# Merging two gathered 64x64 layers: M in eight 64x32 tiles, W1 turned in two column tiles, x's products in half units

## The reference

```python
def cond(x, index, weights):                       # x (128, 64, 512)
    return jnp.einsum('bct,bcd->bdt', x, weights[index])
x = x + cond(x, itok_B_0_7, L0_cond_weights)       # 8 x 64 x 64
x = x + cond(x, itok_B_1_198, L1_cond_weights)     # 200 x 64 x 64
```

## Time and profile before

| | |
|---|---|
| median of 3 runs | 99.78 us (99.7 to 100.39) |
| the profiled execution | 100.29 us, of which the span is 97.4 us |
| PE busy | 69.0 us (71%) |
| DVE busy | 67.6 us (69%) |
| ACT busy | 54.8 us (56%) |
| POOL busy | 31.8 us (33%) |
| DMA | 35.90 MB, mean 369 GB/s |

### The profile page before, as it was taken

The page is one execution under the profiler, slowest core; times in us unless marked ns, Lnnn a source line. Parts: engine busy times, 40 slices in busy tenths (PEclk is TensorE's granted clock), DMA queues, the critical chain, the costliest instruction groups (busy, mean ns, idle before and its releaser), DMA issues.

```text
span 97.4 us, 2078 instructions
## 1 busy us (share of the span) xinstructions
PE 69.0 (71%) x708; PEld 37.3 (38%) x708; DVE 67.6 (69%) x111; ACT 54.8 (56%) x105; POOL 31.8 (33%) x135
## 2 busy tenths in 40 slices
PE   0400007997799999699699699979969969998000
PEld 0200006996782382265147138236414613322000
DVE  4293000588088889979979988997997997977900
ACT  2200000356277689759939938965992993955800
POOL 2400001888788788787758300000000000000000
PEclk9999999999999999999999999999999999999965
DMA  1999999999999999999999999999998984877975
GB/s 25 339 416 453 422 412 410 410 407 416 405 409 405 410 407 409 409 407 405 407 405 408 372 407 410 405 410 406 401 407 346 391 303 167 314 274 274 380 278 203
DMA packets 13243, 35.90 MB, mean 369 GB/s; under 512 B 689, under 2 KB 818, under 8 KB 13106
## 3 DMA queue, kind: packets, MB, share of 16 engines
q1 hardware_dynamic: 12944, 33.56, 88.5%
q0 software_dynamic: 144, 2.10, 5.0%
q10 hardware_dynamic: 146, 0.13, 0.4%
HBM read 19.01 MB, written 16.78 MB: 367 GB/s over the span
## 4 chain that ended last, share of the span: by engine, by line
PE 37%; DVE 34%; DMA 14%; issue 8%; DVEq 1%
PE psum L202 28%; DVE xy L242 21%; DVE m L236 12%; DMA w_rows<-in_L_cond_weights_dram,cond 12%; PE psum L171 8%; DMA cond<-in_itok_B_dram 3%; PE psum L183 2%; DVE w L222 1%; DVEq L58 1%; DVE w_rows L276 0%
## 5 line engine op out<-in xcount | busy, mean ns | idle before, releaser
L242 DVE COPY xy<-psum 64x512 f32<-64x512 f32 x64 | 43.8, 684 | 7.5 <-PE psum L202 5.8
L202 PE MATMUL psum<-xy,m 32*64 32x512 f32 x512 | 44.6, 600 | 5.1 <-DVE xy L242 5.1
L242 ACT COPY xy<-psum 64x512 f32<-64x512 f32 x64 | 37.2, 582 | 15.2 <-PE psum L202 13.8
L151 POOL COPY w0t_diag<-w0t 64x64 f32 x128 | 30.0, 234 | 19.9 <-issue 12.6
L202 PEld LDWEIGHTS psum<-xy,m 32*64 32x64 f32 x512 | 14.2, 130 | 29.9 <-DVE xy L242 18.4
L183 PEld LDWEIGHTS psum<-w,w0t_diag 128*128 128x128 f32 x128 | 14.8, 192 | 6.4 <-POOL w0t_diag L151 2.4
L183 PE MATMUL psum<-w,w0t_diag 128*128 128x64 f32 x128 | 15.7, 277 | 1.3 <-DVE w L222 1.3
L171 PE MATMUL psum<-ident,w_rows 128*64 128x128 f32 x64 | 8.5, 301 | 10.7 <-DVE w_rows L276 10.7
L236 DVE COPY m<-psum 32x256 f32<-32x256 f32 x32 | 13.3, 416 | 3.7 <-PE psum L183 2.8
L222 ACT COPY w<-psum 64x512 f32<-64x512 f32 x8 | 4.6, 578 | 17.3 <-PE psum L171 17.3
L236 ACT COPY m<-psum 32x256 f32<-32x256 f32 x32 | 11.7, 365 | 3.1 <-PE psum L183 2.4
(11 more groups left out here) (5 smaller groups left out, 0.6 us busy)
## 6 DMA issues: line engine op xcount, KB each, us to landing
xy<-in_x_dram SPq DMA_DIRECT2D x16, 1024.0 KB, 19.5
out_dram<-xy SPq DMA_DIRECT2D x16, 1024.0 KB, 8.6
w_rows<-in_L_cond_weights_dram ACTq DMA_DIRECT2D x1, 128.0 KB, 2.6
cond<-in_itok_B_dram SPq DMA_DIRECT2D x1, 0.5 KB, 2.5
subjects<-in_itok_B_dram ACTq DMA_DIRECT2D x1, 0.5 KB
w_rows<-in_L_cond_weights_dram,cond POOLq DMA_INDIRECT x1, 11.5
```

The source lines that it names most:

```text
L151: nc.gpsimd.tensor_copy(w0t_diag[rows, g % D_RING, n // 2, h * C:(h + 1) * C], w0t[rows, bass.ds(picked[n] * C, C)]).then_inc(s_w0_diag, 1)
L202: last = nc.tensor.matmul(psum[columns, (SLOT * v + r) % Y_BANKS, :], m[rows, g % M_RING, 2 * v + w - g * GROUP, j, :], xy[rows, 2 * v + w ...
L242: copy(xy[HALVES[r % 2], 2 * v + w, (r // 2) * T:(r // 2 + 1) * T], psum[HALVES[w], (SLOT * v + r) % Y_BANKS, :]).then_inc(done, 1)
```

## The change

POOL no longer writes blocks with zeros. It copies each batch's W0 as it is into `w0b` (128 copies of 64x64 again, no ring; a batch with odd = 0 on partitions 0 to 63, odd = 1 on 64 to 127, where odd is now which four of the unit's eight). DVE's two memsets go. W1 is turned by plain products with the identity as the moving operand, 64 columns each: 128 of them, half writing partitions 0 to 63 and half 64 to 127, so a turn comes out in one copy of 128 partitions. M of a batch is made in products of 64 rows, 32 columns, 64 moving: 16 to a unit on eight array tiles. M is taken out for a block of 1, 3, 4, 4 and 4 units (`BLOCKS`) by one copy on each of DVE and ACT. x's products come in steps of half a unit (8 products, four array tiles, one of three pairs of banks). `cond`'s DMA moves from SP's queue, ahead of x, to ACT's, ahead of W0. The list of registers for POOL is read before the wait for the gather.

```diff
-            for g in range(GROUPS):
-                if g >= D_RING:
-                    pool.wait_ge(s_m_psum, g - D_RING + 1)
...
+            for first in range(0, B, 2 * UNIT):
...
+                if first == 0:
+                    pool.wait_ge(s_gather, 16)
+                    pool.wait_ge(s_w0t, 4)
+                for n in range(2 * UNIT):
+                    v, odd, r = (first + n) // UNIT, n // SLOT % 2, n % SLOT
+                    nc.gpsimd.tensor_copy(w0b[HALVES[odd], v * SLOT + r, :],
+                                          w0t[HALVES[odd], bass.ds(picked[n] * C, C)]).then_inc(s_w0b, 1)
...
+            of = ident[:, :].rearrange("q (v o r) -> q o v r", o=2, r=SLOT)
...
-                    last = nc.tensor.transpose(psum[0:C, bank, (z % 4) * B:(z % 4 + 1) * B],
-                                               w1_rows[:, :, n * TURN + z], ident[:, :])
+                    for odd, rows in enumerate(HALVES):
+                        last = nc.tensor.matmul(psum[rows, n % W1_RING, z * C:(z + 1) * C],
+                                                w1_rows[:, :, n * TURN + z], of[:, odd, :, :],
+                                                start=True, stop=True)
...
+            def products(k):
+                first, n = BLOCKS[k]
+                pe.wait_ge(s_w0b, UNIT * (first + n))
+                if k >= 1:
+                    pe.wait_ge(s_m_v, k)
+                    pe.wait_ge(s_m_s, k)
+                for v in range(first, first + n):
+                    for j in range(J):
+                        for r in range(SLOT):
+                            for odd, rows in enumerate(HALVES):
+                                at = (v % M_COLUMNS * J + j) * C
+                                last = nc.tensor.matmul(psum[QUARTERS[r], M_BANK + odd, at:at + C],
+                                                        w0b[rows, v * SLOT + r, j * Q:(j + 1) * Q],
+                                                        w1[rows, v * SLOT + r, :], start=True, stop=True)
+                last.then_inc(s_m_psum, 1)
+            def apply(k):
+                first, n = BLOCKS[k]
...
+                for v in range(first, first + n):
+                    pe.wait_ge(s_x[v], 16)
+                    for a in range(2):
+                        step = 2 * v + a
+                        if step >= Y_RING:
+                            pe.wait_ge(s_y_v, 2 * (step - Y_RING + 1))
+                            pe.wait_ge(s_y_s, 2 * (step - Y_RING + 1))
+                        for j in range(J):
+                            for h in range(2):
+                                r = 2 * a + h
...
+                        last.then_inc(s_y_psum, 1)
...
+        def copy_y(eng, copy, done, odd, step):
+            v, a = step // 2, step % 2
+            eng.wait_ge(s_y_psum, step + 1)
+            if a == 0:
+                eng.wait_ge(s_y_psum, step + 2)
+            for h in range(2):
+                copy(xy[HALVES[h], 2 * v + odd, a * T:(a + 1) * T],
+                     psum[HALVES[odd], 2 * (step % Y_RING) + h, :]).then_inc(done, 1)
...
+            for k, (first, n) in enumerate(BLOCKS):
+                for step in range(2 * first, 2 * (first + n)):
+                    copy_y(eng, copy, y_done, odd, step)
+                if k + 2 < len(BLOCKS):
+                    copy_m(eng, copy, m_done, odd, k + 2)
```

More of the change, by code:

```diff
@@ L106, in _ @@
         def _(sp):
[L107 to L120, removed]
+            for v in range(UNITS):
+                sp.dma_start(xy[:, 2 * v:2 * v + 2, :], x_view[:, 2 * v:2 * v + 2, :]).then_inc(s_x[v], 16)
+            for v in range(UNITS):
+                sp.wait_ge(s_y_v, SLOT * (v + 1))
+                sp.wait_ge(s_y_s, SLOT * (v + 1))
+                sp.dma_start(out_view[:, SLOT * v:SLOT * (v + 1), :],
+                             xy[:, 2 * v:2 * v + 2, :].rearrange("q s (h t) -> q (s h) t", h=2)
+                             ).then_inc(s_out[v], 16)
+            for v in range(UNITS):
+                sp.wait_ge(s_out[v], 16)
         @block.gpsimd
@@ L173, in _ @@
                 last.then_inc(s_w1_turned, 1)
[L175 to L181, removed]
-                for k in range(GPAIRS):
-                    last = nc.tensor.matmul(psum[:, M_BANK + g % M_RING, k * C:(k + 1) * C],
-                                            w0t_diag[:, g % D_RING, k, :], w1[:, g * GPAIRS + k, :],
-                                            start=True, stop=True)
-                last.then_inc(s_m_psum, 1)
@@ new lines, in apply @@
+            def apply(k):
+                first, n = BLOCKS[k]
+                pe.wait_ge(s_m_v, k + 1)
+                pe.wait_ge(s_m_s, k + 1)
+                for v in range(first, first + n):
[8 more added lines that the diff above has]
+                                r = 2 * a + h
+                                for odd, columns in enumerate(HALVES):
+                                    last = nc.tensor.matmul(psum[columns, 2 * (step % Y_RING) + h, :],
+                                                            m[QUARTERS[r], odd, v % M_RING, j, :],
+                                                            xy[QUARTERS[r], 2 * v + odd, j * T:(j + 1) * T],
+                                                            start=j == 0, stop=j == J - 1)
+                        last.then_inc(s_y_psum, 1)
@@ new lines, in copies @@
+        def copies(eng, copy, w1_done, m_done, y_done, odd):
+            for n in range(odd, TURNS, 2):
+                copy_w1(eng, copy, w1_done, n)
+            copy_m(eng, copy, m_done, odd, 0)
+            copy_m(eng, copy, m_done, odd, 1)
+            for k, (first, n) in enumerate(BLOCKS):
[3 more added lines that the diff above has]
+                    copy_m(eng, copy, m_done, odd, k + 2)
```

116 lines of the change are left out of this document (32 added, 84 removed).

## The result

The changed kernel takes 110.25 us in the median (109.21 to 111.33), the kernel before 100.09 beside it; the ratio is 1.0995 (95% interval 1.088 to 1.111). Forecast were 98.0 us and at most 101.5. The profiled execution of the changed kernel took 111.33 us with a span of 109.5. Some executions of either kernel take longer, mostly at a lower mean granted clock (the profiled one is such a one, with 0.939 against 0.960 to 0.973 in the other three), and in this document medians count them while ratios leave them out.

A forecast was written before the change was run, and what follows sets the result against it. DVE and its hand-over to PE bound the kernel. Unit 1 at 38.9, 14 units of 3.48 and m copies reach 87.8; last copies 2.83, output 4.82: span 95.4, profiled 98.3, median 97.8, plus 0.2: 98.0 us (95.2 to 101.5).

The forecast's parts named there:

- The bound and the hand-over: Steady stage: DVE and its hand-over to PE bound it; period falls from 4.04 to 3.48 us a unit, M's copies nearly hidden.
- M's products in 64x32 tiles: M for four units: 128 records on eight tiles, 16 a tile at 0.057 us, so 0.9 us.
- the cover of 1.3: Steady stage: up to 1.3 us of M's products hide in PE's wait for DVE; anything past that delays the kernel.
- The rival built on it: M's 64x32 tiles overlap only in part: 3.6 us for four units, about 104.5 us in all; chance 0.12.
- 0.115 if the tiles overlap, 0.23 if not: W1's turning: us for a pair of 64-column products, two records on each of two tiles, against 0.106 a transpose before.
- my worst bound: W1's turning: 0.23 us for a pair of products if the two tiles do not overlap.
- a sign of being wrong: Start: the prediction called itself wrong if W1's turning lasts past 33 us.
- The wait for POOL: Start: PE waits about 5 us before M for block 2, until POOL's 64th copy, at 0.292 us a copy.
- The 34.4 of the sum: Start: time in us at which PE goes on after POOL's 64th copy, 33.85 plus 0.5 for the later gather.
- between 0 and about 1 us: Start: cost of cond's tiny descriptors taking turns with x's packets on another queue; net +0.5 us taken.
- The clock after a rest: After the 5 us stall on POOL, TensorE resumes at the lower clock level, costing 1.3 us together.
- the third rival: Longer stall, dearer M products (1.5 to 2 us for four units) or slow instruction fetching: 98.8 to 101 us; chance 0.18.

The follow-up runs named there:

- experiment 11: Changed kernel with cond first on SP's queue and W1 turned by transposes, each transpose then replaced by two 64-column products on one column tile: 114.65 us (one execution).
- experiment 3: Changed kernel with the weights of W1's turning read as 64 neighbouring elements instead of one in every 64; output differs: 110.13 us (one execution).
- experiment 5: Changed kernel with two edits undone, cond first on SP's queue again and W1 turned by transposes as before: 106.10 us, ratio 1.062 to the kernel before.
- Experiment 2: Changed kernel with a plain half of the identity as moving operand of W1's turning instead of stepped runs of 4; output differs: 109.70 us (one execution).
- experiment 9: Kernel before with only x's products in half units (8 products, three bank pairs, one semaphore count a step): 105.76 us, ratio 1.053.
- 6: Kernel of experiment 5 with M made for blocks of 1, 1 and then 2 units: 103.86 us, ratio 1.038 to the kernel before.
- experiment 12: Kernel of experiment 5 with x's loads held back, 7 units at the start and one behind each output: 106.34 us (one execution).
- 13: Changed kernel with cond first, transposes, blocks of 1, 1, then 2 units, and x's products in whole units as before: 103.44 us, ratio 1.037 to the kernel before.
- experiment 7: Changed kernel with M made for blocks of 1, 1 and then 2 units as its only edit: 104.27 us, ratio 1.043 to the kernel before.

## Why the prediction was wrong, step by step

- **The bound and the hand-over: right.** The period is 3.53 us (3.48 said), M's copies take 0.69 and hide. From unit 1 to unit 15 it was 50.94 us where 48.9 were said: 0.05 more a unit, and the rest in block 3.
- **M's products in 64x32 tiles: right in pace.** 32 records in 0.46 us, less the 0.236 that one lasts, over 31 are 0.007 apart, so a round of the eight tiles takes 0.058 (0.057 said). In a row of 128 it is more: 1.48 us less 0.24 are 1.24 where 0.9 were said, just within the cover of 1.3. The Trainium skill ("TensorE: Matmul & The Clock Gate", Part 3, The mechanism) says that weight loads overlap running matmuls only where the row group differs. This does not hold here: the first 32 loads, on two row halves, go through in 0.33 us, while one record lasts 0.236, and two stepped loads on two column tiles of the same rows take 0.147 where one after the other they take 2 x 0.112 (experiment 11). The rival built on it fell.
- **"0.115 if the tiles overlap, 0.23 if not": the step that failed first.** I halved a load of 128 neighbouring columns and forgot that these weights lie 64 elements apart. It measures 0.295 us for a pair of products, four records (18.9 us / 64), above my worst bound. I took 0.115 and put the stage at 0.5 us more than the 8.5 of before, so 9.0; it was 18.9, and its end at 37.5 is past the 33 us that I had named as a sign of being wrong. With neighbouring weights the same pair takes 0.11 (experiment 3, once the pace has settled), so it is the addresses that I had wrong and not the overlap of the tiles.
- **The wait for POOL: there was none.** POOL made its copies at 26.77 / 128 = 0.209 us and not 0.292, and the turning was so late that PE never met it. With the turning undone it would not have met it either: in experiment 5 the copies start at 14.92 at the same pace, so the 64th is there at about 28.3 (an estimate), and PE comes to M for block 2 at 34.07. The 34.4 of the sum stood on this wait.
- **`cond`: "between 0 and about 1 us", taken as 0.5. Measured 2.8**, and 3.3 with the gather.
- **The clock after a rest: right in kind, but not each time**, and from another rest: in the profiled execution a low stretch of 6.6 us stands behind the 2.7 us stall. Experiment 2 has the stall and not the fall. Not foreseen are falls without a long rest (experiment 9).
- **Instructions fetched too slowly** stood in the third rival, which ended at 101 us in all. It is the largest cost left once the turning is undone: experiment 5 has 5.5 us of rests at two places and the clock's falls behind them.

In the sum, unit 15's first y copy was put at 87.8 and came at 101.89 in the profile, 14.1 us later. Unit 0's products of x started at 40.29 and not at about 27.5: about 12.8 late, 2.8 of them from `cond` and the gather and 9.9 from the turning. From there to unit 1's first copy were 10.7 us and not 11.4, a stall on instructions in place of the one on POOL. The other 2.0 are the steady stage.

Two costs hide each other, which is why undoing the turning seemed worth nothing: with it, PE reaches its dense part late, when the loads of x are nearly through; without it, early, when they are in full flow. How far the two levels of the clock and the rests each count in experiments 5, 6, 12 and 13 is not separated.

## What to carry to other kernels

Count the instructions of the engine that does the work, and where they stand: a burst that is cheap in array time can be dear in fetching, above all while the DMAs are full of loads. Look at the addresses of weights, not only at their number, before halving a measured load. And ask first whether a copy can be put where it hides: moving two of four copies gave 3.6% here with no copy added, where a rebuilt kernel lost 10%.

## What the runs showed of the hardware that was not expected

- PE stops after fixed counts of its own instructions, about 256 apart (records 221, 349, 477, 605, with their weight loads), though not at each of them: for 1.4 to 3.5 us while the DMAs are full of loads and the records come thick, 0.4 and 1.4 us in the run where they were idle (experiment 12), not at all in another (experiment 11), and about 1 us farther on in most runs.
- 64 float32 weights for each of 128 rows, 64 elements apart: 0.112 us a load on one tile, 0.147 for two at once on two column tiles, the same from the first records on; neighbouring ones: 0.056 for two once the pace has settled, about 0.106 in the first 2.64 us.
- A 512-byte load of 4-byte pieces landed in 2.4 to 2.5 us in front of x on one queue, and in 5.2 beside x on another.
- POOL's copies of 64x64 came every 0.209 us in the changed kernel and every 0.292 in the one before, at 0.24 us each; no run was made on why.
- TensorE's mean granted clock was 0.87 to 0.91 in all six executions of a kernel with half the array tiles in use at a time (experiment 9), and in its trace fell twice with no rest over 0.65 us ahead of it since 29 us; another kernel with the same half units kept it up from 20 to 95 us (experiment 7).
